# Top-2 mixture of experts on a graph layer: the gate folded into a tile's products, the steps of a tile moved apart, and one idle product of TensorE per chunk

## The reference

```python
h = feats * rsqrt(deg_out)[:, None]
m = segment_sum(h[src], dst) * rsqrt(deg_in)[:, None]
x = (m @ W_gc + b_gc) + (feats @ W_res + b_res)
logits = x @ Wg + bg                       # 64 experts
vals, idx = top_k(logits, 2); gates = softmax(vals)
core = sum over the two experts: gate * (gelu(x @ w1 + b1) @ w2 + b2)
y = batch_norm(x + core) * gamma + beta
out = layernorm(feats + y)
```

## Time and profile before

| | |
|---|---|
| median of three runs | 3894.4 us (3894.08 to 3895.22) |
| the profiled execution | 3930.65 us |
| its span | 3928.9 us |
| mean granted clock of PE in the span | 0.898 |
| gathers of `aggregate` | 1,661 |

### The profile page before, as it was taken

One profiled execution on the slowest core, in us unless ns is written; L12 is line 12 of the kernel. 1 busy time (PEld: TensorE's weight loads), 2 busy tenths in 40 slices (PEclk: granted clock), 3 DMA queues, 4 the chain that ended last, 5 costly groups with the idle time before them and its releaser, 6 DMA issues. The chain is left out here.

```text
span 3928.9 us, 62567 instructions
## 1 busy us (share of the span) xinstructions
PE 3072.2 (78%) x16322; PEld 2275.8 (58%) x16486; DVE 1928.6 (49%) x6495; ACT 1147.8 (29%) x2819; POOL 2086.8 (53%) x2177
## 2 busy tenths in 40 slices
PE   4636787888888788887888878887799999999650
PEld 3523455555555555555555555555599989889540
DVE  6971344444444444434444444443655555555487
ACT  3950111111111111111111111111344444444228
POOL 3006666666666666666666666665255555555400
PEclk8867889989989999899998998889899999999885
DMA  8534344343434344343434434333444454444477
GB/s 355 196 131 123 103 116 116 105 116 105 116 106 115 109 112 114 104 116 106 116 106 115 117 106 115 106 105 91 126 147 137 146 168 134 144 145 137 124 250 222
DMA packets 288815, 522.53 MB, mean 133 GB/s; under 512 B 44699, under 2 KB 189982, under 8 KB 285968
## 3 DMA queue, kind: packets, MB, share of 16 engines
q0 software_dynamic: 102048, 274.24, 25.4%
q1 hardware_dynamic: 183888, 207.62, 16.4%
q10 hardware_dynamic: 2720, 38.64, 2.3%
HBM read 404.64 MB, written 120.48 MB: 134 GB/s over the span
## 5 line engine op out<-in xcount | busy, mean ns | idle before, releaser
L1167 POOL DMA_INDIRECT work<-h_table,src_cols x1661 | 1572.5, 947 | 1085.7 <-issue 396.3
L1470 PE MATMUL ps<-work 128*128 128x257 f32 x3322 | 1091.6, 408 | 135.9 <-issue 132.4
L1470 PEld LDWEIGHTS ps<-work 128*128 128x128 f32 x3322 | 644.7, 205 | 381.6 <-issue 215.2
L1376 PE MATMUL ps<-none_w,none 128*128 128x512 bf16 x2213 | 730.3, 406 | 58.9 <-issue 53.7
L1721 PEld LDWEIGHTS ps<-xst,work 128*128 128x128 f32 x3648 | 443.3, 192 | 29.7 <-issue 18.8
L1721 PE MATMUL ps<-xst,work 128*128 128x128 f32 x3648 | 447.4, 276 | 12.2 <-issue 12.2
L1604 POOL DMA_INDIRECT picked<-ys,places x232 | 256.3, 1105 | 352.0 <-DVE ys L1674 330.1
L1728 PE MATMUL ps<-work,hid 128*128 128x256 f32 x1824 | 436.1, 382 | 0.2
L1187 DVE TENSOR_TENSOR work<-rel_cols,ps 128x1152 f32<-128x1152 f32 x196 | 250.9, 1281 | 301.8 <-PE ps L1470 230.7
L1376 PEld LDWEIGHTS ps<-none_w,none 128*128 128x128 bf16 x2344 | 237.1, 104 | 273.4 <-issue 134.3
L1585 ACT ACTIVATE hid<-ps,b_cols 128x128 f32<-128x128 f32 x912 | 300.0, 366 | 194.0 <-PE ps L1721 145.8
(11 more groups left out here) (261 smaller groups left out, 3892.1 us busy)
## 6 DMA issues: line engine op xcount, KB each, us to landing
work<-in_L_gnn_w_dram SPq DMA_DIRECT2D x128, 512.0 KB
work<-h_table,src_cols POOLq DMA_INDIRECT x1661
picked<-acc ACTq DMA_DIRECT2D x1, 25088.0 KB, 102.0
pk<-picked SPq DMA_DIRECT2D x14, 1792.0 KB
m_base<-acc ACTq DMA_DIRECT2D x1, 12642.0 KB, 36.9
acc<-m_base SPq DMA_DIRECT2D x14, 903.0 KB
x_rows<-acc SPq DMA_DIRECT2D x98, 129.0 KB
x_beta<-xr_x SPq DMA_DIRECT2D x98, 128.0 KB
```

What stands on the lines that cost most here:

```text
L1167: pool.indirect_dma_start(out=got[:, c % RING, 0:D], out_offset=None, in_=h_table[:, :], in_offset=bass.IndirectOffsetOnAxis(ap=src_cols[: ...
L1376: nc.tensor.matmul(ps[:, 7, :], none[:, :], none_w[:, :], start=False, stop=False)
L1470: nc.tensor.matmul(ps_flat[:, bank(t, k, w[0])], hot[:, (2 * t + (k >= HALF)) % HOTS, k % HALF if k >= HALF else k, :], got[:, c % RING, : ...
```

## The change

1. **The gate is folded.** `w_conv`, `w_res` and the bias rows get 64 more columns, which hold W Wg. The five products of `product` are 320 columns wide instead of 256 and give x1 and the logits together. `turn_x1`, `gate`, `keep_x1_turned` and their semaphores are gone. The folded columns are made once, in slot 1: `turn_weights` (14 transposes) and `fold_weights` (10 small products), with DVE copies between them, in tiles at the end of `acc` that are not in use yet.
2. **The steps are moved.** `turn_in` to chunk 3 (lag 2), `ranks` to chunk 13 (lag 3), `product` to chunk 15 (lag 2), `list_places` to chunk 16 (lag 4). The ranks go to bank 6, so that `product` no longer waits for `ranks_set`; it waits for `x1_set` and `logits_set` of the tile before it. In DVE's slot `choose` and `place` now stand ahead of `evict`. ACT's order in a slot is `keep_x1`, `keep_turned`, `odds_of`, `root_of`, `mean_in`.
3. **Idle products.** `IDLE` is 1 instead of 2, and three chunks instead of five have none.

```diff
-        LIST_AT, TURN_AT, TURN_X1_AT, RANKS_AT, PRODUCT_AT, GATE_AT = 1, 2, 4, 6, 11, 13
-        TURN_LAG, PRODUCT_LAG, TURN_X1_LAG, GATE_LAG, RANKS_LAG, LIST_LAG = 2, 2, 3, 3, 4, 5
-        BUSY = (TURN_AT, PRODUCT_AT, TURN_X1_AT, GATE_AT, LIST_AT)
-        IDLE = 2
+        TURN_AT, FOLD_AT, RANKS_AT, PRODUCT_AT, LIST_AT = 3, 12, 13, 15, 16
+        TURN_LAG, PRODUCT_LAG, RANKS_LAG, PLACE_LAG, LIST_LAG = 2, 2, 3, 4, 4
+        BUSY = (TURN_AT, PRODUCT_AT, LIST_AT)
+        DX = D + X
+        IDLE = 1
...
                 for slot in range(1, NT + DRAIN):
-                    for lag, f in ((TURN_LAG, keep_turned), (TURN_X1_LAG, keep_x1_turned), (1, root_of), (PRODUCT_LAG, keep_x1),
-                                   (1, mean_in), (GATE_LAG, odds_of)):
+                    for lag, f in ((PRODUCT_LAG + 1, keep_x1), (TURN_LAG, keep_turned), (RANKS_LAG, odds_of), (1, root_of), (1, mean_in)):
...
                 def choose(t):
-                    dve.wait_ge(logits_done, t + 1)
-                    nc.vector.tensor_tensor(logits[:, :], ps[:, 6, D:D + X], gate_bias[:, :], ALU.add).then_inc(logits_set, 1)
+                    dve.wait_ge(x1_set, t + 1)
+                    nc.vector.tensor_tensor(logits[:, :], ps[:, 5, D:DX], gate_bias[:, :], ALU.add).then_inc(logits_set, 1)
...
+                    if within(slot - RANKS_LAG):
+                        choose(slot - RANKS_LAG)
+                    if within(slot - PLACE_LAG):
+                        place(slot - PLACE_LAG)
                     if within(slot - 1):
                         evict(slot - 1)
                         degree(slot - 1)
...
-                    if within(slot - RANKS_LAG):
-                        place(slot - RANKS_LAG)
                     if slot + 2 < NT:
                         one_hots(slot + 2, 0)
                     if within(slot - 1):
                         degree_factor(slot - 1)
-                    if within(slot - GATE_LAG):
-                        choose(slot - GATE_LAG)
-                        add_x1(slot - GATE_LAG)
+                    if within(slot - RANKS_LAG):
+                        add_x1(slot - RANKS_LAG)
...
                     if t > 0:
                         pe.wait_ge(x1_set, t)
-                    if t >= RANKS_LAG - PRODUCT_LAG:
-                        pe.wait_ge(ranks_set, t - (RANKS_LAG - PRODUCT_LAG) + 1)
+                        pe.wait_ge(logits_set, t)
+                    else:
+                        pe.wait_ge(folded, 1)
                     for k in range(KD):
-                        nc.tensor.matmul(ps[:, 5, 0:D], turned[:, k, :], w_conv[:, k, :], start=(k == 0), stop=False)
+                        nc.tensor.matmul(ps[:, 5, 0:DX], turned[:, k, :], w_conv[:, k, :], start=(k == 0), stop=False)
...
-                def turn_x1(t):
-                    pe.wait_ge(x1_set, t + 1)
...
-                def gate(t):
-                    pe.wait_ge(x1t_kept, t + 1)
...
                 def ranks(t):
                     pe.wait_ge(route_hot_set, t + 1)
-                    pe.wait_ge(x1_set, min(t + RANKS_LAG - PRODUCT_LAG, NT))
...
+                    nc.tensor.matmul(ps[:, 6, 0:X], lower_b[:, :], route_hot[:, t % 2, :], start=True, stop=False)
+                    nc.tensor.matmul(ps[:, 6, 0:X], ones_b[:, :], seen[:, t % 2, :], start=False, stop=True).then_inc(ranked, 1)
...
+                def turn_weights():
+                    pe.wait_ge(wr_in, 112)
...
+                def fold_weights():
+                    pe.wait_ge(b1_kept, 1)
+                    for n in range(2 * KD):
+                        for o in range(KD):
+                            nc.tensor.matmul(ps[:, 6, n * X:(n + 1) * X], fold_t[:, n // KD, n % KD, o, :], w_gate[:, o, :],
+                                             start=(o == 0), stop=(o == KD - 1))
...
                         if t == 1 and k == TURN_AT:
...
+                            turn_weights()
+                        if t == 1 and k == FOLD_AT:
+                            fold_weights()
+                end(NT - 1)
                 for k in STEPS_AT:
                     if k >= len(chunks(NT - 1)):
                         step(k, NT - 1)
-                end(NT - 1)
```

More of the change, by code:

```diff
@@ L968, in aggregate @@
         turned = t2("turned", [P, 2 * KD, P], F32)
-        x1t = t2("x1t", [P, KD, P], F32)
         lower_b = t2("lower_b", [P, P], BF16)
@@ L1115, in _ @@
                         keep_x_beta(slot - 2)
-                    if within(slot - RANKS_LAG):
-                        store(slot - RANKS_LAG)
+                    if within(slot - PLACE_LAG):
+                        store(slot - PLACE_LAG)
                 for u in range(1, HELD - 1):
@@ L1308, in _ @@
                         one_hot_x(slot + 1)
+                    if slot == 1:
+                        dve.wait_ge(wr_in, 112)
+                        dve.wait_ge(b1_turned, 1)
+                        nc.vector.tensor_copy(spare[:, 0:F1], ps_flat[:, 5 * BANK:5 * BANK + F1])
+                        nc.vector.tensor_copy(spare[:, F1:F2], ps[:, 4, KH * X:KH * X + F2 - F1])
+                        nc.vector.tensor_copy(b1_cols[:, :, :], ps[:, 4, 0:KH * X].rearrange("p (h e) -> p h e", e=X)).then_inc(b1_kept, 1)
+                    if slot == 2:
+                        dve.wait_ge(folds_done, 1)
+                        for w, kept in enumerate((w_conv, w_res)):
+                            nc.vector.tensor_copy(kept[:, :, D:DX], ps[:, 6, w * KD * X:(w + 1) * KD * X].rearrange("p (k e) -> p k e", k=KD))
+                        nc.vector.tensor_copy(bias_rows[:, D:DX], ps[0:2, 6, 2 * KD * X:(2 * KD + 1) * X]).then_inc(folded, 1)
+                    if within(slot - RANKS_LAG):
+                        choose(slot - RANKS_LAG)
+                    if within(slot - PLACE_LAG):
+                        place(slot - PLACE_LAG)
                     if within(slot - 1):
@@ L1311, in _ @@
                         degree(slot - 1)
-                    if slot == 1:
-                        dve.wait_ge(wr_in, 112)
-                        dve.wait_ge(b1_turned, 1)
-                        nc.vector.tensor_copy(b1_cols[:, :, :], ps[:, 4, 0:KH * X].rearrange("p (h e) -> p h e", e=X)).then_inc(b1_kept, 1)
-                    if within(slot - RANKS_LAG):
-                        place(slot - RANKS_LAG)
                     if slot + 2 < NT:
@@ L1440, in list_places @@
                     mm.then_inc(listed, 1)
-                STEPS_AT = {LIST_AT: (list_places, LIST_LAG), TURN_AT: (turn_in, TURN_LAG), TURN_X1_AT: (turn_x1, TURN_X1_LAG),
-                            RANKS_AT: (ranks, RANKS_LAG), PRODUCT_AT: (product, PRODUCT_LAG), GATE_AT: (gate, GATE_LAG)}
+                STEPS_AT = {TURN_AT: (turn_in, TURN_LAG), RANKS_AT: (ranks, RANKS_LAG), PRODUCT_AT: (product, PRODUCT_LAG),
+                            LIST_AT: (list_places, LIST_LAG)}
                 def step(k, slot):
@@ L1490, in _ @@
                             pe.wait_ge(seen_set, NT)
-                            nc.tensor.matmul(ps[:, 5, D + X:D + 2 * X], ones_b[:, :], seen[:, NT % 2, :], start=True, stop=True).then_inc(counted, 1)
+                            nc.tensor.matmul(ps[:, 6, X:2 * X], ones_b[:, :], seen[:, NT % 2, :], start=True, stop=True).then_inc(counted, 1)
 def experts(nc, x1_rows, picked, w1s, w2s, b2s, w_in, load_weights, ident, table, base_of, b1_cols, y_total, ps, D, X, H, KD, KH, ROW, PLACES):
```

65 lines of the change are left out of this document (31 added, 34 removed).

## The result

| | before | changed |
|---|---|---|
| median of 9 runs each | 3894.94 us (3891.12 to 3897.61) | 3884.99 us (3881.40 to 3891.71) |
| ratio | | 0.9976, 95% interval 0.9967 to 0.9985 |
| the profiled execution | 3930.65 us | 3884.45 us |
| its span and mean clock | 3928.9 us, 0.898 | 3882.5 us, 0.866 |

A forecast was written before the change was run, and what follows sets the result against it. PE's lateness was taken to hold POOL's gathers above their 21.2 us a tile; at 21.7 the stage falls 315 us to 2120, with 15 to 20 at the end: 3894.4 - 333 = 3561, say 3560, range 3500 to 3890.

The forecast's parts named there:

- POOL's floor: Gather stage: POOL's own cycle of 1.247 us a gather, 21.2 us a tile, is the floor under any gain on PE.
- PE's work: Gather stage: PE's own work per tile falls from 17.6 to 15.3 us at full clock, 16.8 at 0.91.
- The wait on `ranks_set` goes, and no new wait comes: Before `product` on PE: 2.4 us a tile gained, the moved steps having over 6 us to spare.
- the unknown: Gather stage: what POOL at full pace does to PE; 0.5 us a tile taken, range 0 to 2.3.
- The lateness belongs to the gathers: PE's completion signals lag typically 4 to 5 us while gathers are issued, and no longer after the last one.
- Fewer idle products leave PE room: Idle products per tile go from 24 to 14, 2.15 us less; a reason to take only 0.5 us lost.
- The tail: Between last gather and experts, 65.7 us: PE fewer chunks behind POOL, up to 19 us less, 15 taken.
- The clock: PE's clock stays near 0.9 with one idle product; 0.85 or more in the stage was the sign.
- The low-clock rival: Mean PE clock under 0.61 makes PE's tile pass 25.0 us; at 0.55, 4150 us in total. Chance 0.11.
- lag of 3.7 us: PE's signal lag as a 64-entry queue draining: 8 entries a chunk becoming 6 shortens 4.9 to 3.7 us; not summed.
- the third: Rival: gathers set PE's standing time whatever it has queued; tile stays 25.0 us, total 3885 to 3895. Chance 0.06.
- The fourth: Rival: DVE's `choose` and `place` ahead of `evict` delay it if `product`'s signal is over 10 us late; 3990. Chance 0.04.

The follow-up runs named there:

- Prompt jobs: Jobs where the unaltered kernel before takes 3551.95 to 3559.28 us; ACT's copy of x1 starts 0.04 us after `product`'s modelled end.
- e11: The kernel before, unaltered, traced in a prompt job: 3561.56 us.
- late jobs: Jobs where the unaltered kernel before takes 3894.94 to 3923.25 us; ACT's copy of x1 starts a median 6.4 us or more after `product`'s modelled end.
- e1: Changed kernel with no gathers after the 38th and no waits for them, prompt job: 2985.23 us.
- e6: Changed kernel with POOL gathering into places PE does not read, neither waiting for the other, late job: 5110.42 us, beside 3923 for the kernel before.
- e15: Changed kernel with no idle products (`IDLE` 0), late job: 3901.66 us, 0.9949 of the kernel before.
- e8: Changed kernel with no idle products (`IDLE` 0), prompt job: 1.0029 of the kernel before.
- e7: Changed kernel with PE signalling `summed` only at every second chunk, prompt job on chip 4: 1.0007 of the kernel before.
- e14: Changed kernel with PE signalling `summed` only at every second chunk, late job on chip 4: 3912.42 us, 0.9977 of the kernel before.

## Why the prediction was wrong, by its steps

- **POOL's floor**, 1.247 us a gather and 21.2 a tile: right. Prompt jobs with gathers of 128 rows run at 1.250 to 1.259: the kernel before (e11) and the changed kernel with its small edits. Without an edit the changed kernel ran in late jobs only.
- **PE's work**, 15.3 us a tile: right (e1, at most 16.0).
- **The wait on `ranks_set` goes, and no new wait comes**: right as far as it went. The wait of `product`'s first weight loads fell from 208 to 9.7 us.
- **The step that failed** is the one headed as the unknown, what a POOL at full pace does to PE. I took 0.5 us a tile over 21.2, with 2.3 as the upper end; it was 3.4 (24.6). Behind it stood two sentences. One bound let PE keep "(5.6 - 2.4) + 16.8 = 20.0, which is still under 21.2": it took PE's standing time as a fixed sum from which a removed wait can be subtracted. But POOL pauses only when PE is late, and in late jobs PE becomes late because of POOL's gathers. PE's 15.3 us at a clock of 0.85 are 18.0, so it now stands 6.6 us of 24.6, one more than before. PE's matmuls sat idle for 178 us less before `product` (180.1 in the trace of before, 1.8 now), and for 136 us more before the chunks' products (242.7 now; the row of before is below) and some 60 more before `list_places`: the wait went elsewhere. The other sentence was "a wait that a signal of 4.9 us ends is removed whatever makes it late": true of that wait, and beside the point.
- **The lateness belongs to the gathers**: right, and e6 shows it far more strongly than the earlier trace rows. I read the crawl in the earlier trace rows, then sized it by the 4.4 us that POOL waited once after it. PE's rate there was the number to carry on: 38 matmuls in 23 us, where the kernel before in the prompt job has 87 (e11). The group of the chunks' products in 400 to 2600 us, and the first ring, both of the kernel before:

```profile
L1470 PE MATMUL ps<-work 128*128 128x257 f32 x2992 | 977.3, 405 | 106.5 <-issue 103.5
...
312.00:335.00 23.00, 10.21 (x38) 5.68 (x37) 1.35 (x1) 0.00 (x0) 17.40 (x19) 0.71 0.38 109
```

- **Fewer idle products leave PE room**: wrong. None moved the time by 0.3% at most, and twice as many, seen in a prompt job only, not at all.
- **The tail**, 15 us less: 14.0 in the profiles. That is as large as the whole gain of 10 to 14 us in the medians, and in prompt jobs the tail is 43 us with the kernel before (e11) and 43 to 47 with the changed kernel's edits. That the tail is all of the gain is argued from these sizes; no run isolates it.
- **The clock** stayed, 0.85 in the stage for a forecast of 0.85 or more. The low-clock rival fell; even at 0.79 (e15) nothing was lost. The estimate from the Trainium skill ("TensorE: Matmul & The Clock Gate", the table at its head) of a lag of 3.7 us had the wrong sign: with fewer instructions the lag grew. But the queue of 64 entries that the Trainium skill's table gives TensorE agrees with the count of 62 or 63 instructions in e6, and no late trace exceeds it; the error was to turn entries into time at an undisturbed rate. The section "Why this matters for your kernels" of the same page of the Trainium skill asks for matmuls without long gaps between bursts. That does not foresee e8: only 4 idle times of PE's matmuls in 400 to 2200 us are longer than 2 us there, the longest 2.96 (in e7 2 of them, the longest 2.13), and yet the mean clock is 0.85, where it is 0.99 with one idle product (e7). At a pace that POOL sets, that cost 0.3% at most.
- **The rivals**: the third, that PE's standing time is set by the gathers and the tile stays, 3885 to 3895, is what happened in late jobs. I gave it 0.06. Against it I put that a removed wait is removed; for it stood the one observation that decides, that the lag ends with the gathers (within some 9 us after the last, in the coupled traces). The fourth, DVE as the wait, had its condition (a lag of `product`'s signal over 10 us) in 21 of 93 tiles, but no idle time of PE in the stage is put down to DVE. That 3885 lies inside the range of 3500 to 3890 is no merit of the mechanism: the range was stretched over a part of the unchanged case, and the time came out 5 us inside its end.

What stays open: what makes a job late, and which part of a gather holds TensorE back, as the hold outlasts both the issuing and the transfer (e6). One rival was not tested. Every timed execution of the experiments has a recorded clock, the late traces lack the gathers' landings, and no execution without recording stands beside them; so the recording itself may have a part in the lateness. Both kinds issue the same instructions and the same bytes, and chip 4 was of both. Whether a smaller window or smaller gathers help there was not seen, since those runs fell on prompt jobs.

## What to carry to other kernels

Before subtracting a wait from an engine's idle time, ask whether that idle time is fed back: if A waits for B because A's own issuing slows B, a wait removed from B can return elsewhere, and an uncoupled run (e6) shows it. Price such an interference by the rate of the slowed engine while the other runs, not by one pause. And take the kernel before once more in another job before explaining a stall: here the 334 us that the profile showed as a stall of TensorE were a condition of the job, and in the other kind of job neither the kernel before nor the edited changed kernel has them.

## What the runs showed of the hardware

- In some jobs a GpSimd that issues indirect gathers without a pause brings TensorE down to one instruction per gather (1,485 beside 1,511) and its clock to 0.50 (e6). In other jobs TensorE's signal comes 0.04 us after its modelled end beside gathers at 1.25 us each (e11). Chip 4 had a job of either kind (e7 and e14).
- In e6 TensorE stays at that pace for 27 us after GpSimd's last gather, for the last 20 of them with no DMA traffic of the core.
- In the late traces a signal of TensorE follows its matmul by up to 63 instructions, in e6 by 62 or 63 (86 us) in each of the 10 tiles looked at.
- The uncoupled GpSimd is slowed as well, 1.39 us a gather instead of 1.25.
- An indirect gather costs 1.25 us of GpSimd for 128 rows of 1,024 bytes, 1.25 for 128 of 512 bytes, and 1.21 for 64 of 1,024 bytes.
